# Weighting the values with the probabilities as the stationary operand, in a gated cross-attention and feed-forward block

## The reference

```python
def xattn(memory, query, seq_mask, b):          # memory: [4,512,512], query: [4,512,256]
    K, V = split(memory, 2, axis=2)             # into 8 heads of 32
    logits = einsum('bhqd,bhkd->bhqk', Q * 32 ** -0.5, K) + b[0]
    logits = logits + -1e30 * (1.0 - seq_mask)  # over the memory rows
    return einsum('bhqk,bhkd->bhqd', softmax(logits), V)

def ffn(x, w_gate, w_up, w_down):               # int32 weights / 127, hidden 768
    return (silu(x @ wg.T) * (x @ wu.T)) @ wd.T

x = x + tanh(g_xattn) * xattn(ctx, layernorm(x), mask)
x = x + tanh(g_ffn) * ffn(layernorm(x), ...)
```

## Time and profile before

| what | us |
|---|---|
| median of 3 runs | 151.34 (151.26 to 153.39) |
| the profiled execution, its own time | 151.04 |
| its span, from the first to the last instruction | 149.2 |
| busy: PE, DVE, POOL, ACT | 128.0, 107.9, 108.0, 91.0 |
| TensorE's granted clock, mean | 1.000 of full speed |

### The profile page before, as it was taken

The page is one execution under the profiler, slowest core; times in us unless marked ns, Lnnn a source line. Parts: engine busy times, 40 slices in busy tenths (PEclk is TensorE's granted clock), DMA queues, the critical chain, the costliest instruction groups (busy, mean ns, idle before and its releaser), DMA issues.

```text
span 149.2 us, 3758 instructions
## 1 busy us (share of the span) xinstructions
PE 128.0 (86%) x1283; PEld 96.5 (65%) x1283; DVE 107.9 (72%) x283; ACT 91.0 (61%) x202; POOL 108.0 (72%) x157
## 2 busy tenths in 40 slices
PE   0899586999697997899989997999899899699970
PEld 0346363676365784799866975887586788587860
DVE  4989799999925993799758677696673977546722
ACT  3235998798495865744567858675686544475500
POOL 7478948779899999978871378949649679876600
PEclk9999999999999999999999999999999999999999
DMA  4599999184700499640230020300300532200222
GB/s 148 148 332 371 370 208 121 37 161 89 143 0 4 79 201 173 129 90 23 67 57 0 7 70 0 75 0 4 69 1 0 40 107 70 71 6 0 70 81 77
DMA packets 30976, 13.80 MB, mean 93 GB/s; under 512 B 24532, under 2 KB 30184, under 8 KB 30952
## 3 DMA queue, kind: packets, MB, share of 16 engines
q1 hardware_dynamic: 30912, 13.51, 39.8%
q10 hardware_dynamic: 40, 0.01, 0.0%
HBM read 5.52 MB, written 2.10 MB: 51 GB/s over the span
## 4 chain that ended last, share of the span: by engine, by line
POOL 41%; PE 22%; DVE 14%; issue 8%; DMA 7%; ACT 6%; SPq 1%; DVEq 0%; ACTq 0%; POOLq 0%
POOL norm L651 13%; PE ps L1406 8%; PE ps L1430 6%; POOL rstd L629 5%; POOL x_sb L668 5%; POOL q_parts L658 5%; DVE stats L923 5%; POOL h L675 4%; DMA n_t<-norm 4%; POOL norm L658 4%; DMA x_sb<-in_x_dram 3%; DVE gated L1107 2%; DVE h L1118 2%; PE ps L1338 2%; ACT norm L711 2%
## 5 line engine op out<-in xcount | busy, mean ns | idle before, releaser
L1406 PE MATMUL ps<-n_t,w_gu_t 128*128 128x256 f16 x384 | 47.6, 273 | 3.1 <-DVE h L1118 1.9
L1406 PEld LDWEIGHTS ps<-n_t,w_gu_t 128*128 128x128 f16 x384 | 36.0, 98 | 11.0 <-DVE h L1118 4.0
L675 POOL TENSOR_TENSOR h<-h 128x256 f16<-128x256 f32 x48 | 31.4, 673 | 9.0 <-ACT h L833 8.8
L1107 DVE SCALAR_TENSOR_TENSOR gated<-tanh_h,ps 128x256 f32<-128x256 f32 x48 | 19.9, 415 | 15.1 <-ACT tanh_h L824 14.7
L1430 PE MATMUL ps<-w_d_t,h 128*128 128x256 f16 x192 | 24.7, 273 | 0.9 <-DVE x_sb L900 0.9
L824 ACT ACTIVATE tanh_h<-ps 128x256 f32<-128x256 f32 x48 | 18.0, 380 | 12.2 <-PE ps L1406 11.9
L1063 DVE TENSOR_REDUCE max_cols<-ps 128x4 f16<-128x512 f32 x32 | 20.7, 682 | 4.6 <-PE ps L1263 4.4
L1118 DVE SCALAR_TENSOR_TENSOR h<-ps,gated 128x256 f32<-128x256 f32 x48 | 20.4, 424 | 4.5 <-POOL h L675 2.8
L776 ACT ACTIVATE probs<-ps,exp_bias 128x512 f32<-128x512 f32 x32 | 20.8, 686 | 3.3 <-PE ps L1310 3.0
L833 ACT ACTIVATE h<-h 128x256 f16<-128x256 f32 x48 | 19.0, 412 | 4.5 <-DVE h L1118 3.6
L1430 PEld LDWEIGHTS ps<-w_d_t,h 128*128 128x128 f16 x192 | 18.2, 98 | 4.0 <-issue 2.0
(11 more groups left out here) (97 smaller groups left out, 183.7 us busy)
## 6 DMA issues: line engine op xcount, KB each, us to landing
x_sb<-in_x_dram SPq DMA_DIRECT2D x8, 256.0 KB, 8.7
out_dram<-x_sb SPq DMA_DIRECT2D x8, 256.0 KB, 2.2
kv<-in_ctx_dram SPq DMA_DIRECT2D x4, 256.0 KB, 6.3
w_raw<-in_L_ffn_w_gate_dram SPq DMA_DIRECT2D x1, 768.0 KB, 7.9
w_raw<-in_L_ffn_w_up_dram SPq DMA_DIRECT2D x1, 768.0 KB, 9.6
w_raw<-in_L_ffn_w_down_dram SPq DMA_DIRECT2D x1, 768.0 KB, 9.5
q_stacks<-q_parts SPq DMA_TRANSPOSE x12, 3.3
n_t<-norm SPq DMA_TRANSPOSE x6, 3.2
```

The source lines that it names most:

```text
L675: pool.tensor_tensor(h16[:, r % 2, m, 1, :], h32[:, n % NHB, :], h16[:, r % 2, m, 0, :], ALU.subtract).then_inc(h_low, 1)
L1107: mine(dve.scalar_tensor_tensor(out=gated[:, n % 2, :], in0=tanh_h[:, n % 2, :], scalar=1.0, in1=got[:, 0:SH], op0=ALU.add, op1=ALU.mult))
L1406: ins = pe.matmul(dst, lhs, rhs, start=(w == 0 and (k, l) == terms[0]), stop=(k, l) == terms[-1], skip_group_check=True)
```

## The change

The weighting of the narrow program is turned round. `weigh_o`, `weigh_d` and `o_copy` no longer occur in it. `attn_t` now runs, for a query tile, 8 f32 matmuls (one a head) with a 128x128 block of `probs` (keys by queries) as the stationary operand and 33 columns moving: the 32 value columns of the head and a column of ones, whose product is the sum. The values are copied into that layout (`v_ones`, pitch `V_COLS` = 34, in the memory of `o_sb`) by a new ACT step `vc` (`v_copy`), one for each batch element; POOL sets the ones at the start. The exp of a score step waits for the second `attn_t` of the half two before. Bank 4 is a third `WORK` bank.

On GpSimd the norm is computed as (x + (-mean)) x deviation instead of (x - mean) x deviation, with `neg_mean` from an added 128x2 instruction in each `stats` step whose norm POOL does (10 of them).

`ones_b` is the first constant to be written, and 14 warm-up matmuls start behind it alone; 25 more stand in 8 places of PE's order. The orders of all engines are new; PE's is shown up to the first hidden step and beyond it.

```diff
-WARM_UP = (8, 2, 4, 4, 9, 3)
+WARM_UP = (4, 3, 3, 3, 3, 3, 3, 3)
+FIRST_WARM_UP = 14
+V_COLS = DH + 2
...
 ORDER = {
     "sp": """
-        qn2 wn0 qn3 wn1 qn4 nn1 wn2 qn5 qn6 nn2 qn7 fi0 nn3 fi1 nn4 nn5 nn6 fi2 fi3 fi4 fi5 fi6 fi7""",
+        qn2 qn3 wn0 wn1 wn2 qn5 qn4 nn1 qn6 nn2 qn7 fi0 nn3 nn4 fi1 nn5 nn6 fi2 fi3 fi4 fi5 fi6 fi7""",
     "pe": """
...
+        wu7 ks0 wu0 qs0.0 wu5 qs0.1 wu1 rm0.0 rm0.1 qs1.0 wu3 rm0.2 rm0.3 rm1.0 qs1.1 wu6 mt rm1.1 mx0 rm1.2 rm1.3 sc0.0
+        sc0.1 wu4 sc0.2 sc0.3 wu2 ks1 mx1 at0.0 at0.1 sc1.0 sc1.1 rm2.0 rm2.1 sc1.2 rm2.2 sc1.3 rm2.3 rm3.0 rm3.1 rm3.2
+        mx2 at1.0 nt0 sc2.0 at1.1 sc2.1 hi0.0 hi0.1 sc2.2 rm3.3 sc2.3 hi0.2 hi0.3 hi0.4 hi0.5 at2.0 do0.0 at2.1 hi1.0
+        hi1.1 do0.1 mx3 ft hi1.2 sc3.0 sc3.1 hi1.3 ks2.0 sc3.2 ks2.1 rm4.0 hi1.4 sc3.3 do0.2 rm4.1 hi1.5 rm4.2 rm4.3
...
     "pool": """
+        sa0 la0 sa1 la1 sa2 kp1 na2 sa3 na3 sa4 la2 sa5 sa6 la3 sa7 at0.0 at0.1 la4 sb0 nb0 lb0 la5 at1.0 at1.1 kp2 sb1
+        nb1 lb1 hs0.0 hs0.1 hs0.2 hs0.3 hs0.4 at2.0 at2.1 la6 hs0.5 sb2 nb2 hs1.0 lb2 hs1.1 la7 hs1.2 hs1.3 hs1.4 hs1.5
...
-        WORK, SCORES, O_BANK, HID_BANKS, Y_BANK = (0, 1), (2, 3), 4, (5, 6), 7
+        WORK, SCORES, O_BANK, HID_BANKS, Y_BANK = (0, 1, 4), (2, 3), 4, (5, 6), 7
...
         @block.gpsimd
         def _(pool):
+            pool.memset(ones_b[:, :], 1.0).then_inc(pool_done, 1)
...
+            pool.memset(v_ones[:, :, :, DH:DH + 1].rearrange("p b h d -> p (b h) d"), 1.0).then_inc(pool_done, 1)
...
+                        if step[1] == 2 or norm1_on_pool((step[0].replace("stats", "norm1"), step[2])):
+                            pool.tensor_scalar(neg_mean[:, place % NLB, :], mv[:, place % NLB, :, 0], -1.0, None, ALU.mult)
...
                             ins = pool.tensor_scalar(norm32[:, slot, i, :], x_sb[:, 2 * r + i, :],
-                                                     mv[:, slot, i, 0:1], rstd[:, slot, i:i + 1],
-                                                     ALU.subtract, ALU.mult)
+                                                     neg_mean[:, slot, i:i + 1], rstd[:, slot, i:i + 1],
+                                                     ALU.add, ALU.mult)
...
-                        if j >= NPB:
-                            act.wait_ge(weighed, (j - NPB) // 2 + 1)
...
+                        elif j >= NPB:
+                            used = (j - NPB) // (2 * NG)
+                            act.wait_ge(work_filled, plan.filled(("attn_t", used // 2, 2 * (used % 2) + 1)))
...
+                    elif kind == "v_copy":
+
+                        b = step[1]
+                        act.wait_ge(kv_loaded[b], 16)
+                        act.activation(v_ones[:, b, :, 0:DH], kv[:, b, D:2 * D].rearrange("p (h d) -> p h d", h=NH),
+                                       ACT.Copy).then_inc(v_ready, 1)
...
+                            heads = got[:, 0:NH * V_COLS].rearrange("p (h d) -> p h d", d=V_COLS)
+                            values = heads[:, :, 0:DH]
+                            mine(dve.reciprocal(recip[:, n % 2, :].unsqueeze(2), heads[:, :, DH:DH + 1]))
...
         @block.tensor
         def _(pe):
+            pe.wait_ge(pool_done, 1)
+            for _ in range(FIRST_WARM_UP):
+                pe.matmul(bank32(Y_BANK), ones_b[:, :], ones_b[:, :].unsqueeze(1).to_broadcast((P, HG, P)),
+                          start=True, stop=True)
             pe.wait_ge(pool_done, CONSTS)
...
+                    elif kind == "attn_t" and not is_wide:
+
+                        _, b, qt = step
+                        n = open_work(step)
+                        j0 = plan.nth["scores", b, qt // 2, 0, LAST, 0]
+                        pe.wait_ge(exp_done, j0 + 2 * NG)
+                        pe.wait_ge(v_ready, b + 1)
+                        for h in range(NH):
+                            at = (h % 2) * SH + (qt % 2) * P
+                            ins = pe.matmul(bank32(n)[:, h * V_COLS:h * V_COLS + DH + 1],
+                                            probs[:, (j0 + h // 2) % NPB, at:at + P], v_ones[:, b, h, 0:DH + 1],
+                                            start=(h == 0), stop=(h == NH - 1), skip_group_check=True)
+                        ins.then_inc(work_filled, 1)
```

More of the change, by code:

```diff
@@ L420, in flamingo_block_kernel @@
         wide = wide_steps(B, MT, NC)
-        plan = Plan(steps + wide, n_early, WORK + HID_BANKS, WORK, emptied_by)
+        plan = Plan(steps + wide, n_early, WORK + HID_BANKS, WORK, WORK[0:2], emptied_by)
         def ln_slot(kind, which, r):
@@ L1317, in run @@
                         values = kind == "weigh_o"
-                        first, last = not is_wide or c == 0, c == LAST
+                        first, last = c == 0, c == LAST
                         j0 = plan.nth[of("scores"), b, half, g, c, 0]
                         pe.wait_ge(exp_done, j0 + 2)
+                        if values and plan.nth[step] == 0:
+                            for read in plan.early_users(O_BANK):
+                                pe.wait_ge(*read)
                         if first or not values:
@@ L1336, in run @@
                             else:
-                                ins = pe.matmul(sums_at(is_wide)[part, :], sum_cols[:, g, :], pr,
-                                                start=(is_wide and g == 0 and c == 0), stop=(last and g == NG - 1),
+                                ins = pe.matmul(sums_wide[part, :], sum_cols[:, g, :], pr,
+                                                start=(g == 0 and c == 0), stop=(last and g == NG - 1),
                                                 tile_position=(0, j * DH), skip_group_check=True)
```

109 lines of the change are left out of this document (52 added, 57 removed), and 2 rows, old and new, of the table CODES.

## The result

The change makes the kernel slower: 177.25 us (median of 4 runs, 177.02 to 177.74) against 151.30, a ratio of 1.170 (95% interval 1.166 to 1.175). I had forecast 147.3 with a range up to 154.0. The profiled execution takes 177.22 us and its span is 173.2; before they were 151.04 and 149.2.

What follows compares the result with a forecast made beforehand. Small DVE, ACT and POOL operations were taken to bound a front of some 43 us, PE the body after it. First hidden 37.1 + body 104.7 + finish 3.4 + 1.84 = 147.0, median 147.3 us; range 138.5 to 154.0.

Steps and rivals of the forecast that it cites:

- the granted clock falls in a stretch of short matmuls ... small: On PE: the clock case, counted as slower than before, chance 0.03; the trace before showed full grant in each stretch.
- the 57 ns: On PE: fast-load rival, 57 ns a pass, attn_t 0.91 us, total 139.8 us; chance 0.25.
- the 139 ns rival: On PE: loads that do not overlap moving, 139 ns a pass, 2.22 us a tile, total 157.8 us; chance 0.14.
- the 141 ns row: Listed 128-column f32 load in the transposes, 57 ns over a one-column load; the low end for a pass.
- 6.0 us more of PE: Weighting on PE: 27.4 us for all 16 tiles against 21.4 before, at 107 ns a pass.
- The whole body run at 95%: From first hidden matmul on: 99.5 us of PE work at 95% fill, 94 for PE's present best, one for the third bank: 104.7 us.
- First hidden at about 37.1: Front: first hidden matmul at about 37.1 us, from 43.15; adds end 4.3 earlier, norm gives 1.5, neg_mean costs 0.1 to 0.2.
- New: attn_t follows the exps at once ... ending near 28.5: Front: exps done at 25.4, then attn_t in 2 x 1.71 us; DVE and POOL, 0.7 each, put the adds' end near 29.9.
- the rival without it: Norm on POOL no faster: front keeps 1.7 us, POOL full to 60 us, fill about 92%, total 152.5 us; chance 0.15.
- The DMAs at nothing: SyncE's queue: reordered q and n transposes cost nothing, up to 0.7 us each where a hidden matmul waits.

Runs made afterwards that it cites:

- ones between the heads: Changed kernel with a 240-column matmul of ones behind each head but the last of a tile, into columns no one reads: 169.93 us, ratio 1.123.
- the weighting alone: Changed kernel, faster norm included, with the orders and warm-ups of before, the old weighting's steps struck out of them: 163.57 us, and 169.28 in the other execution.
- the mixed kernel: Changed kernel with the heads of an attn_t alternating with matmuls of the score, hidden or down step behind it: 171.33 us, and 177.01 in the other execution.
- the held kernel: Changed kernel with matmuls of ones between the heads and more warm-ups in the front's idle stretches, 15 of them ahead of mx1: 166.10 us, ratio 1.091.
- the other order: Changed kernel with n and q transposes ahead of the third weight's on SyncE's queue: 174.36 us, and 177.34 in the other execution.

## Why the prediction was wrong

The loss adds up from the runs, each figure a difference of two of them:

| step | us | from |
|---|---|---|
| before | 151.3 | |
| the norm, with 9 warm-ups, at full clock | -8.0 | 143.3 measured |
| the f32 passes, orders of before, clock full | +14 to +19 | 162.25, less up to 4.5 for the added ones, less 143.3 |
| the new orders at full clock | +3 to +4 | 166.10 - 162.25 |
| the clock | +11 to +16 | 177.25 - 166.10, plus up to 4.5 for the added ones |
| after | 177.3 | the ranges of passes and clock go together: 14 with 16, 19 with 11 |

**The clock: the first step that failed.** I wrote "the granted clock falls in a stretch of short matmuls ... small", with 0.03, because every stretch of the earlier trace rows is at full grant. The rows of before could not bear that out: there 128 to 512 columns move behind nearly every load of 128 columns, and no stretch has a train of loads with 33 columns behind each. The changed kernel shows two triggers: an idle stretch (3.63 us at 25.6) and passes in a row that PE is listed as busy with (12.49 of 12.5 us at 0.59). The runs take them away one at a time: ones between the heads remove the second (7.3 us), warm-ups in the gap with them both (11.1 us, with the added work still in it). My price for a low clock, up to 5 us for 10 us, fits: 30.8 us of it cost 11 to 16. But my sum had no term for it at all; what I took for small was the amount. The runs don't tell more closely what it is in the passes that lowers the clock than this: more columns behind the same f32 loads lower it less. I cannot say from one execution to the next how time follows clock: the changed kernel's four span 0.897 to 0.920 and 0.7 us with no order in it, while the weighting alone has 5.7 us between its two, at 0.957 and 0.917.

The Trainium skill ("TensorE: Matmul & The Clock Gate", section "HAM oscillation — how this bites in real kernels") says that waits between blocks of matmuls bring the throttle back each time. The idle stretch of 3.63 us ahead of the first passes agrees; the fall in the middle of gapless passes at 88.45 to 90.48 is not in that section.

**The passes, on PE: the size right, their worth not.** 107 ns a pass, 1.71 us a tile and 27.4 us in all were right, and so was the overlap with moving: neither the 57 ns nor the 139 ns rival came. The rule of the Trainium skill by which I weighed the load ("TensorE: Matmul & The Clock Gate", section "LDWEIGHTS (loading the stationary operand)") agrees with the 107 ns; the 141 ns row, of a transpose, did not carry over. But I priced 6.0 us more of PE at little more than 6.0 us, and at full clock the weighting cost 14 or more. This is the second step that failed; the next paragraph says what is known of it.

**"The whole body run at 95%" failed.** The kernel with the fast norm and the old weighting nearly does that: 94.03 of 99.7 us listed busy, 94%, from its first hidden matmul at 41.5 to the span's end. With the passes (and the ones between the heads) under the same orders it is 104.67 of 116.1, 90%. A tile of passes keeps PE for 1.71 us, in which ACT and DVE get nothing new of PE (ACT's tanh waits 33.1 us for hidden matmuls after, 11.9 before). I think that this lumpiness is the reason for the lower fill; the mixed kernel, made for it, gave 171.33 and 177.01 us and decides nothing, so it is argued and not shown.

**"First hidden at about 37.1" failed.** It came at 51.35, and at 43.53 with the clock held. Of the 14 us, 7.8 are thus clock and idle stretch. The rest is in the sentence "New: attn_t follows the exps at once ... ending near 28.5". The exps are done at 25.3, but the new list has mx1 ahead of at0.0, and mx1's maxima are reduced by DVE from 27.85 on, behind a copy, statistics and a norm that start at 25.11. In the held kernel the passes start at 28.12 and POOL's adds end at 33.85 where I said 29.9; and ahead of the first hidden step there stand both tiles of block 1's weighting, 2 x 1.71 us of PE, which I had in neither sum. The rows for this were there: the list of the new order stands in the diff. The sum had slips too, all small: by its own terms the first hidden matmul is at 43.15 - 4.3 - 1.5 + 0.15 = 37.5 and not 37.1, 3.42 us behind 25.4 end at 28.8 and not 28.5, and 17 row_max make 3.7 and not 3.9.

**The norm.** The direction was right and the size off: 563 ns, not 420, so 20 x 0.68 = 13.6 us saved and not 16.4, less 2.3 for the negations: 11.3 off POOL (108.0 to 96.6) and not 15. Its worth, by the rival without it, I put at 152.5 - 147.3 = 5.2 us. In the changed kernel it was 4 to 5; on the kernel before it was 5 to 9 alone and 8.0 with the warm-ups. That kernel's chain had POOL at 41% and PE at 22%, and I had read its body as bound by PE alone. The rival that the norm is no faster did not come.

**The DMAs at nothing** missed less: the hidden step waits 4.4 us for n_t in two places after (0.7 before), and the other order gave 0 to 3 us. But such a wait is an idle stretch too, with the clock to pay behind it: 1.5 us more for the 16 hidden matmuls behind the 2.40 us of the held kernel.
